# Two chained attention blocks on one core: the value product turned, the MLP computed by rows

## The reference, cut to what matters

```python
# block 0 (8 heads of 16, 64 sampled keys per image)
x_ln = layernorm(x);  q = x_ln @ wq + bq
# q -> depthwise conv 7x7 stride 2 -> gelu -> offsets -> bilinear sampling of x
k = v = interp @ wv + bv
attn = softmax(heads(q @ mq_w) . heads(k @ mk_w))          # 256 x 64 per head
att  = attn . heads(v @ mv_w)
z    = (att @ mo_w + mo_b) + x
x1   = gelu(layernorm(z) @ mlp_w + mlp_b) + z               # exact gelu
# block 1
xg = groupnorm(x1, 32 groups)                               # statistics over pixels and 4 channels
q, k, v = xg @ wq, xg @ wk, xg @ wv                         # + biases
out = softmax(q k^T / sqrt(128)) v @ wo + bo + x1
```

## Time and profile before

| | |
|---|---|
| median of 3 executions | 72.55 us (72.22 to 74.87) |
| the profiled execution's own time | 73.03 us |
| its span, first to last instruction | 71.2 us |
| granted TensorE clock | 1.00 |
| PE busy | 92% |
| PEld busy | 75% |
| DVE busy | 66% |
| ACT busy | 53% |
| POOL busy | 28% |
| HBM read, written | 2.42 MB, 0.52 MB |

### The profile page before, as it was taken

One profiled execution on the slowest core, in us unless ns is written; L12 is line 12 of the kernel. 1 busy time (PEld: TensorE's weight loads), 2 busy tenths in 40 slices (PEclk: granted clock), 3 DMA queues, 4 the chain that ended last, 5 costly groups with the idle time before them and its releaser, 6 DMA issues.

```text
span 71.2 us, 2063 instructions
## 1 busy us (share of the span) xinstructions
PE 65.6 (92%) x774; PEld 53.1 (75%) x774; DVE 47.0 (66%) x164; ACT 37.6 (53%) x94; POOL 19.9 (28%) x32
## 2 busy tenths in 40 slices
PE   4989789999999999999999999969999999999940
PEld 1316379987867758899889899738888889989730
DVE  0249873105523996679799998899499595375680
ACT  5210349544625686644441598973452949668400
POOL 6001999991000003960000931090300300000000
DMA  0778692000000000000000000000000000002213
GB/s 0 201 238 212 204 390 115 9 0 9 0 9 0 0 0 0 5 0 9 0 0 0 5 9 0 0 0 0 0 0 0 0 9 5 0 0 74 71 49 101
DMA packets 3051, 3.07 MB, mean 43 GB/s; under 512 B 225, under 2 KB 2657, under 8 KB 3042
## 3 DMA queue, kind: packets, MB, share of 16 engines
q1 hardware_dynamic: 3042, 2.95, 13.2%
HBM read 2.42 MB, written 0.52 MB: 41 GB/s over the span
## 4 chain that ended last, share of the span: by engine, by line
PE 83%; DVE 6%; DMA 4%; issue 2%; SPq 1%; DVEq 0%
PE bank L913 47%; PE score L913 22%; PE bank L1095 6%; DMA pack_early<-early 4%; PE score L1245 1%; PE bank L1113 1%; DVE y L779 1%; SPq L268 1%; DVE q_conv L579 1%; PE bank L1245 1%; DVE rec L777 1%; PE score L1164 1%; PE bank L1134 1%; DVE z L698 1%; PE score L1143 1%
## 5 line engine op out<-in xcount | busy, mean ns | idle before, releaser
L913 PEld LDWEIGHTS bank<-v_blk,p_t 128*128 128x128 f32 x64 | 7.8, 192 | 0.9 <-ACT p_t L446 0.7
L913 PE MATMUL bank<-v_blk,p_t 128*128 128x34 f32 x64 | 8.1, 272 | 0.0
L662 DVE TENSOR_REDUCE smax<-score 128x8 f32<-128x512 f32 x8 | 5.5, 686 | 1.6 <-PE score L913 1.6
L446 ACT ACTIVATE p_t<-bank 128x512 f32<-128x512 f32 x8 | 4.8, 599 | 2.7 <-PE bank L1095 2.7
L337 POOL TENSOR_TENSOR zrs<-zve,neg_half 128x2 f32<-128x2 f32 x4 | 2.8, 708 | 12.1 <-DVE zve L710 11.9
L913 PE MATMUL bank<-q_ph,wd 128*32 128x84 f32 (+5 forms) x256 | 6.0, 248 | 0.0
L913 PE MATMUL score<-warm 128*128 128x512 bf16 x12 | 5.0, 561 | 1.0 <-POOL warm L290 1.0
L913 PEld LDWEIGHTS bank<-q_ph,wd 128*32 128x32 f32 x256 | 5.3, 110 | 0.6 <-issue 0.3
L669 DVE TENSOR_TENSOR s_sub<-score,smax 128x512 f32<-128x512 f32 x8 | 5.5, 690 | 0.2
L324 POOL TENSOR_TENSOR x_res<-x_st,msa_bias 128x1024 f32<-128x1024 f32 x1 | 2.4, 2372 | 11.7 <-DVE bilin L642 11.7
L301 POOL TENSOR_TENSOR wd<-pack_early 128x512 f32<-128x512 f32 x4 | 4.1, 1047 | 5.2 <-DVE x_hat L602 5.2
(11 more groups left out here) (186 smaller groups left out, 162.6 us busy)
## 6 DMA issues: line engine op xcount, KB each, us to landing
x_st<-x SPq DMA_DIRECT2D x1, 512.0 KB, 7.3
pack_late<-late SPq DMA_DIRECT2D x1, 448.0 KB, 7.9
out<-y SPq DMA_DIRECT2D x3, 128.0 KB, 1.7
pack_fold<-fold SPq DMA_DIRECT2D x1, 320.0 KB, 4.5
pack_mid<-mid SPq DMA_DIRECT2D x1, 258.0 KB, 6.4
x_hw<-x SPq DMA_DIRECT2D x2, 128.0 KB, 2.6
x_hw<-x SPq DMA_DIRECT2D x1, 256.0 KB, 4.2
pack_early<-early SPq DMA_DIRECT2D x1, 184.0 KB, 2.9
```

Of the source, the lines that this page charges most:

```text
L446: act.activation(p_t[:, i % 2].rearrange("p j q -> p (j q)"), tile_bank(i)[:, :], ACT.Exp).then_inc(s["exp_ok"], 1)
L662: dve.tensor_reduce(smax[:, i % 2].rearrange("p (j e) -> p j e", e=2), scores, AX.X, ALU.max).then_inc(s["smax_ok"], 1)
L913: return pe.matmul(o, l, r_, start=start, stop=stop, **k)
```

## The change

1. **Value product turned.** The value blocks (32 columns) become the stationary operand and `p_t` (128 columns) the moving one; the four head pairs go to four quadrants of 32 partitions. Four more matmuls with a stationary mask of ones give the softmax sums, spread over the same layout. The result has channels on partitions, so `att_transpose` and its copy go. The reciprocal becomes `exp(-ln(sum))` on ACT, in a table set that holds both, loaded once by name where the Exp set was loaded.
2. **MLP by rows.** The weights are centred (`centre @ mlp_wg`), so z itself is multiplied: z is transposed, copied, and is the stationary operand, 128 columns of weights move. The row scale and the bias come after the product (`mlp_rows`, DVE), gelu follows on rows. `zhat_image`, `z_offset` and `zhat_transpose` go.
3. **Gelu transposed onto z.** z's transpose stays in PSUM as an open accumulation; `x1_add` transposes gelu onto it. `x1_image` and `x1_transpose` go; statistics and `norm_image` read PSUM.
4. **Residual rows on POOL** (`residual_rows`, `x1_rows`), in place of `x1_residual` on DVE.
5. **Bias rows** arrive by one broadcast transfer of 192 KB and are added by DVE; the two matmuls against a row of ones that added them go.
6. Group norm: one matmul where there were three ahead of the square; each image has its own bank for MLP, projections and x1; all engines' orders are rewritten.

The core of the diff (the order of each engine's steps is shown from the last tiles of the first attention on; ahead of that the new PE order is score 0, coord 1, query 1, score 1, transposes 0, residual bias, value 0, score 2, sample 1, transposes 1, key 1, score 3, values 1, value 1, transposes 2, score 4, out 0 and 1, value 2, transposes 3, score 5, `centre_weights`, value 3, `fold_second`, score 6, out 2, transposes 4, out 3, transposes 5, score 7):

```diff
             sp.dma_start(packs["mid"][:, :], mid).then_inc(s["mid_in"], 16)
+            sp.dma_start(biases[:, :, :].rearrange("p n c -> p (n c)"), bias_rows.partition_broadcast(P)).then_inc(s["biases_in"], 16)
             sp.dma_start(x_st[:, :, :], x_st_dram).then_inc(s["xst_in"], 16)
             sp.dma_start(packs["late"][:, :], late).then_inc(s["late_in"], 16)
 
+            def residual_rows(b):
+                pool.wait_ge(s["z_ok"], 2 * b + 2)
+                pool.wait_ge(s["outbias_ok"], 1)
+                pool.tensor_tensor(z_out[:, 2 * b:2 * b + 2], z[:, 2 * b:2 * b + 2], out_bias[:, :].unsqueeze(1).to_broadcast([P, S, C]),
+                                   ALU.add).then_inc(s["zout_ok"], 1)
+
+            def x1_rows(b):
+                pool.wait_ge(s["zout_ok"], b + 1)
+                pool.wait_ge(s["gel_ok"], b + 1)
+                pool.tensor_tensor(x1_res[:, 2 * b:2 * b + 2], z_out[:, 2 * b:2 * b + 2], gel[:, 2 * b:2 * b + 2], ALU.add).then_inc(s["x1res_ok"], 1)
...
             z_scale(2)
+            residual_rows(0)
+            residual_rows(1)
             z_scale(3)
             gn_pow(0)
+            x1_rows(0)
+            x1_rows(1)
+            residual_rows(2)
+            residual_rows(3)
             gn_pow(1)
+            x1_rows(2)
+            x1_rows(3)
...
+            def log_tile(i):
+                act.wait_ge(s["av_mm"], i + 1)
                 if i >= 2:
-                    act.wait_ge(s["msa_mm"], i - 1)
-                act.copy(att_t[:, i % 2], tile_bank(i)[:, ATT_T]).then_inc(s["attt_ok"], 1)
+                    act.wait_ge(s["inv_ok"], i - 1)
+                act.activation(log_sum[:, i % 2], tile_bank(i)[:, SUM], ACT.Ln).then_inc(s["log_ok"], 1)
+
+            def inverse_tile(i):
+                act.wait_ge(s["log_ok"], i + 1)
+                if i >= 2:
+
+                    act.wait_ge(s["att_ok"], i - 1)
+                act.activation(inv_sum[:, i % 2], log_sum[:, i % 2], ACT.Exp, scale=-1.0).then_inc(s["inv_ok"], 1)
...
+                act.activation(gel[:, 2 * b:2 * b + 2], mlp_in[:, 2 * b:2 * b + 2], ACT.Gelu).then_inc(s["gel_ok"], 1)
...
-            att_tile(4)
+            log_tile(4)
+            inverse_tile(4)
+            log_tile(5)
+            inverse_tile(5)
             exp_tile(6)
-            zhat_image(0)
             exp_tile(7)
-            zhat_image(1)
-            att_tile(5)
-            act.activation(scratch[:, 3:4], eps[:, :], ACT.Gelu)
             zt_image(0)
             zt_image(1)
+            log_tile(6)
+            log_tile(7)
+            inverse_tile(6)
+            inverse_tile(7)
+            act.activation(scratch[:, 3:4], eps[:, :], ACT.Gelu)
             gelu_image(0)
             gelu_image(1)
-            zhat_image(2)
-            out_bias_copy()
             zt_image(2)
             zt_image(3)
             gelu_image(2)
...
-            def recip_tile(i):
...
             def norm_tile(i):
-                dve.wait_ge(s["recip_ok"], i + 1)
+                dve.wait_ge(s["inv_ok"], i + 1)
...
+                dve.tensor_tensor(att_t[:, i % 2], tile_bank(i)[:, ATT], inv_sum[:, i % 2], ALU.mult).then_inc(s["att_ok"], 1)
...
+            def mlp_rows(i):
+                dve.wait_ge(s["mlp_mm"], i // S + 1)
+                dve.wait_ge(s["zrs_ok"], i // S + 1)
+                dve.wait_ge(s["mlpbias_ok"], 1)
+                dve.scalar_tensor_tensor(out=mlp_in[:, i], in0=image_bank(i // S)[:, i % S * C:(i % S + 1) * C], scalar=zrs[:, i:i + 1],
+                                         in1=mlp_bias[:, :], op0=ALU.mult, op1=ALU.add).then_inc(s["mlpin_ok"], 1)
...
+            def gn_mean(n):
+                i = slice(GN_SETS[n].start, GN_SETS[n].stop)
+                dve.wait_ge(s["dev_mm"], n + 1)
+                dve.tensor_tensor(gmean[:, i], gmv[:, i, 0], gn_bank(n)[:, DEV][:, i], ALU.subtract).then_inc(s["gmean_ok"], 1)
...
+            max_tile(7)
+            shift_tile(7)
+            z_aggr(1)
             z_stats(2)
-            z_tile(3)
             norm_tile(4)
-            max_tile(7)
+            norm_tile(5)
...
+            z_var(0)
             z_var(1)
+            z_tile(5)
...
+            mlp_rows(0)
             z_var(2)
+            norm_tile(6)
+            mlp_rows(1)
+            norm_tile(7)
+            mlp_rows(2)
+            mlp_rows(3)
             z_tile(6)
+            z_stats(6)
+            out_bias_out()
             z_tile(7)
-            z_stats(6)
-            z_stats(7)
-            z_aggr(6)
-            z_aggr(7)
-            z_offset(2)
-            z_var(3)
-            x1_image(0)
-            x1_image(1)
             gn_stats(0)
             gn_stats(1)
             gn_aggr(0)
             gn_aggr(1)
-            zhat_image(3)
+            z_aggr(6)
+            z_stats(7)
+            z_aggr(7)
+            z_var(3)
             gn_square(0)
+            gn_mean(0)
+            mlp_rows(4)
+            mlp_rows(5)
             gn_var(0)
+            mlp_rows(6)
+            mlp_rows(7)
             norm_image(0)
-            x1_residual(1)
             norm_image(1)
-            x1_image(2)
-            x1_image(3)
             gn_stats(2)
             gn_stats(3)
             gn_aggr(2)
             gn_aggr(3)
             query_out(0)
+            gn_mean(1)
+            gn_square(1)
             query_out(1)
-            gn_square(1)
-            x1_residual(2)
-            x1_residual(3)
             gn_var(1)
             norm_image(2)
+            max_image(0)
             norm_image(3)
-            max_image(0)
             max_image(1)
             query_out(2)
             query_out(3)
...
+                for at, stationary in ((ATT, v_blk[:, b]), (SUM, None)):
+                    for j in range(PAIRS):
+                        v = w("ones_mask") if stationary is None else stationary[:, j]
+                        m = mm(tile_bank(i)[j * VW:(j + 1) * VW, at], v, p_t[:, i % 2, j])
...
+                pe.wait_ge(s["ssub_ok"], T)
                 for t in range(S):
-                    m = pe.transpose(zt_bank(b)[:, HW + t * P:HW + (t + 1) * P], z[:, 2 * b + t], w("ident"))
+                    m = mm(x1_cols(b)[:, t * P:(t + 1) * P], z[:, 2 * b + t], w("ident"), start=(t == 0), stop=False, is_transpose=True, skip_group_check=True)
                 m.then_inc(s["zr_mm"], 1)
...
+                pe.wait_ge(s["mlpwc_ok"], 1)
+                for t in range(S):
+                    m = mm(image_bank(b)[:, t * C:(t + 1) * C], z_t[:, 2 * b + t, :], mlp_wc[:, :], start=False, skip_group_check=True)
+                m.then_inc(s["mlp_mm"], 1)
...
+            def x1_add(b):
+
+                pe.wait_ge(s["gel_ok"], b + 1)
                 for t in range(S):
-                    m = pe.transpose(bank[3 + b][:, HW + t * P:HW + (t + 1) * P], x1_t[:, b, t * P:(t + 1) * P], w("ident"))
-                m.then_inc(s["x1rows_mm"], 1)
+                    m = mm(x1_cols(b)[:, t * P:(t + 1) * P], gel[:, 2 * b + t], w("ident"), start=False, is_transpose=True, skip_group_check=True)
+                m.then_inc(s["x1_mm"], 1)
+
+            def gn_apart(n):
                 i = slice(GN_SETS[n].start, GN_SETS[n].stop)
                 pe.wait_ge(s["gmv_ok"], i.stop)
                 if n == 0:
...
+                mm(gn_bank(n)[:, DEV][:, i], w("group_rest"), gmv[:, i, 0]).then_inc(s["dev_mm"], 1)
...
+            score_tile(7)
             value_tile(4)
+            value_tile(5)
             transpose_scores(6)
-            att_transpose(4)
-            value_tile(5)
+            z_transpose(0)
+            transpose_scores(7)
             out_project(4)
-            transpose_scores(7)
+            z_transpose(1)
+            out_project(5)
             value_tile(6)
-            att_transpose(5)
+            mlp_image(0)
+            mlp_image(1)
+            z_transpose(2)
             out_project(6)
             out_project(7)
             output_bias()
-            gn_mean(0)
+            x1_add(0)
+            x1_add(1)
+            z_transpose(3)
+            mlp_image(2)
+            gn_apart(0)
+            mlp_image(3)
             gn_spread(0)
+            x1_add(2)
+            x1_add(3)
             project_k(0)
             project_q(0)
+            project_k(1)
+            gn_apart(1)
             project_q(1)
-            x1_transpose(2)
-            x1_transpose(3)
-            project_k(1)
-            gn_mean(1)
             project_v(0)
             gn_spread(1)
             score_image(0)
             score_image(1)
+            project_v(1)
             project_q(2)
```

More of the change, by code:

```diff
@@ L23 @@
 PIX = OH * OW
-VW = 2 * HD + 2
+VW = 2 * HD
 LN_EPS, GN_EPS = 1e-5, 1e-6
@@ L66, with build @@
 PLACE = {pack: columns(parts) for pack, parts in PACKS.items()}
-def build(nc, x, early, fold, mid, late, rows, ln_rows, out):
+def build(nc, x, early, fold, mid, late, rows, ln_rows, bias_rows, out):
     ctx = ExitStack()
@@ L187, in build @@
```

(41 more changed lines are left out.)

392 lines of the change are left out of this document (164 added, 228 removed).

## The result

| | before | after |
|---|---|---|
| median of 4 executions each | 72.64 us (72.22 to 74.87) | 75.17 us (75.09 to 76.48) |
| ratio, 95% interval | | 1.033 [1.028, 1.038] |
| span of the profiled execution | 71.2 us | 73.0 us |
| its own time | 73.03 us | 75.16 us |
| granted TensorE clock | 1.00 | 0.95 |

The forecast was 69.8 us within 67.6 to 72.4. Of most kernels here single executions are some per cent slower than the rest, mostly at a lower clock; ratios leave them out, medians don't, and where a kernel has no ratio its lowest time is given.

The account below looks back on a forecast made before the run. It saw a loop set by a single score buffer, then serial chains, then dense PE work, rather than PE alone. Stage gains took 2.7 us off the 71.2 us span; from the 72.55 median this gave 69.8 us, range 67.6 to 72.4.

Parts of the forecast that it names:

- the one on POOL: Residual rows on POOL: eight operations of 256 columns at 0.61, 4.9 us, hidden if the powers behind them are not late.
- the term for tile 2: First attention: value product 0, the bilinear step and the bias sums hold DVE until 27.9 instead of 28.2.
- The slower rival (ACT's order): First attention: logs ahead of later exps delay each exp and stall the loop, 6.4 us over 6 tiles; 74.7 us, 7%.
- Packed value product: First attention on PE: turned product of 16 instructions takes 0.55 us per tile instead of 0.82, saving 3.4 us with att's transpose.
- the second rival: Score loop on PE: changeovers of packing, 0.11 us paid twice per tile, add 1.8 us; 71.6 us, 20%.
- Work of the engines: Whole kernel: PE loses 5.6 us of work, DVE ends about 3 us lighter, POOL gains 4.9 us.
- ACT's chain: After the first attention: exp, copies, log, inverse and an exposed 1.28 us table load lead to gelu at 45.3; gain 1.5.
- The power of the second half: Second group norm on POOL: `gn_pow(1)` stands behind four residual operations until 52.3, in time by 1.2 us.
- Loop: First attention's score rounds, set by a single score buffer: 2.21 us each, last subtraction ending at 40.3 instead of 41.5.
- The same work in another order: Stretch up to the first scores: only reordered, so they come at 22.4 instead of 22.45.
- Outside the span: Time of the profiled execution beyond its span: 1.8 us, kept unchanged.

Follow-up runs that it names:

- e1: The changed kernel with POOL's wait for the second bilinear step put back ahead of `x_res`; 71.67 us, ratio 0.986 to the kernel before.
- e3: The kernel before with only POOL's wait for the second bilinear step ahead of `x_res` taken out; 76.42 us, ratio 1.035.
- e11: The changed kernel, no wait put back, with `x_res` made in four operations of 256 columns instead of one of 1024; 72.58 us, ratio 0.991.

## Why the prediction was wrong

**The step that failed** is the one on POOL. The prediction costed POOL's eight new operations (4.9 us, hidden) and nothing else of that engine's list. That `x_res` no longer waited for the bilinear product was not in it, as a gain or as a risk, nor which DVE operation would run beside it. In the sum this is the term for tile 2: there the bilinear step and the bias sums were to hold DVE until 27.9, and they held it until 30.2, because the bilinear step took 2.56 us and not the 0.42 that it had before (29.94 + 0.28; 28.20 in e1). And no term allowed for a slower clock. That is 2.1 us of stall and 2.1 us of clock, 4.1 of the 4.5 us between the forecast span of 68.5 and the measured 73.0. The slower rival (ACT's order) gave 74.7, near the time that came, but only by chance; it is not what happened: only the two rounds in the hole and the slow clock are above 2.4 us (27.22 to 32.59 to 36.02), and behind them the rounds are 2.25, 2.21 and 2.38, in e1, with ACT's order the same, 2.32, 2.21 and 2.38. The Trainium skill states the rule in SBUF — State Buffer (Who interferes with whom): a DVE instruction with two SBUF inputs contends with a GpSimd one that reads SBUF. It calls this an exclusive lock, and says of DVE's two-port modes that the other engine blocks for the whole instruction; the traces show that for this pair too, 0.28 or 0.29 us between the two ends in four traces.

**The rest of the path came within 0.5 us of the forecast,** read in e1, where the collision is absent; times are of the profiled executions:

| stage | before | forecast | e1 | after |
|---|---|---|---|---|
| first scores | 22.45 | 22.4 | 22.78 | 22.66 |
| last subtraction ends | 41.52 | 40.3 | 40.81 | 44.89 |
| gelu of image 0 | 46.76 | 45.3 | 45.64 | 49.73 |
| first normalized image | 51.49 | 50.0 | 50.20 | 54.27 |
| image 2 normalized | 56.96 | 54.5 | 54.70 | 58.77 |
| scores of images 0 and 1 done | 57.64 | 54.9 | 55.29 | 59.36 |
| span | 71.2 | 68.5 | 68.9 | 73.0 |

The lines of the changed kernel behind the last column, DVE, ACT and PE, which answer to the earlier trace rows:

```profile
44.20 0.69 DVE L704 TENSOR_TENSOR s_sub<-score,smax 128x512 f32<-128x512 f32 x1
...
54.27 0.99 DVE L783 TENSOR_SCALAR x_gn<-score,gmean,grs 128x256 f32<-128x256 f32 x2 [0.32 <-POOL grs L351]
...
58.77 0.55 DVE L783 TENSOR_SCALAR x_gn<-score,gmean,grs 128x256 f32<-128x256 f32 x1 [0.89 <-POOL grs L351]
```
```profile
47.80 0.50 ACT L489 ACTIVATE inv_sum<-log_sum 128x128 f32<-128x128 f32 x2
48.32 1.28 ACT L576 ACT_TABLE_LOAD   x1
...
49.73 0.71 ACT L497 ACTIVATE gel<-mlp_in 128x256 f32<-128x256 f32 x2
```
```profile
57.55 1.97 PE L930 MATMUL bank<-k,q 128*128 128x256 f32 x8
59.36 0.61 PE L930 MATMUL bank<-w_vog,x_gn 128*128 128x128 f32 x4
```

Point by point:

- *Packed value product, 0.55 forecast, bounds 0.45 and 1.81.* It is 0.46, next to the lower bound. PE, products of tiles 4 and 5 in the changed kernel:

```profile
43.29 0.42 PE L930 MATMUL bank<-p_t,v_blk 128*32 128x128 f32 x8
43.53 0.40 PE L930 MATMUL bank<-p_t,pack_mid 128*32 128x128 f32 x8
43.75 0.40 PE L930 MATMUL bank<-p_t,v_blk 128*32 128x128 f32 x8
43.97 0.40 PE L930 MATMUL bank<-p_t,pack_mid 128*32 128x128 f32 x8
44.30 0.66 PE L1116 MATMUL bank<-pack_early,s_sub 128*128 128x128 f32 x4
```

  From start to start 0.24, 0.22, 0.22, 0.33: a product alone 0.46, and 0.11 more where full transposes follow, as much as the second rival priced a changeover. Whether it is one was not tested; with it the product costs 0.57 at most, the forecast's 0.55, and the rival's extra 1.8 us is not there: the loop of e1 is 0.1 us longer than forecast, see below.
- *Work of the engines.* e1's page, against the earlier trace rows:

```profile
PE 61.6 (89%) x820; PEld 47.3 (69%) x820; DVE 45.0 (65%) x152; ACT 36.7 (53%) x95; POOL 25.3 (37%) x39
```

  PE has 4.0 us less where 5.6 were counted, DVE 2.0 less where 3 were, POOL 5.4 more where 4.9 were. The missing 1.6 of PE are not traced to single products, and as busy times of pipelined matmuls they are rough.
- *ACT.* Log 0.28 as assumed, inverse 0.31. One table load ahead of the first exp (24.37) and the one ahead of gelu, in the open with ACT's chain intact (47.80, 48.32, 49.73), as forecast; logs and exps alternate with no load between. The chain came 0.3 late.
- *POOL.* A residual operation of 256 columns takes 0.70 to 0.73, not 0.61. The power of the second half still comes in time.
- *DVE.* Normalizing from PSUM takes 0.54 where it took 0.41 from SBUF; not in the sum, 0.1 on the path.
- *Loop.* Of the 0.5 us by which the last subtraction ends late in e1, 0.4 are there at the first scores already (22.78 against 22.4); the loop itself takes 18.03 against 17.9. "The same work in another order" was not free: from `move_half(1)` to the first scores it takes 8.65 us in e1 (22.78 − 14.13) and 7.65 before (22.45 − 14.80), of which the gap behind 109 tap products is 0.67. That the first scores are late by only 0.4 is luck: what lies ahead of `move_half(1)` was 0.67 shorter in that execution.
- *Outside the span* 1.8 was kept. e1's profiled execution took 71.40 us where 70.3 was forecast: 0.4 of it in the span, 0.7 outside.

So with its one wait the change does to the span most of what was forecast, 2.3 us of 2.7, and its time falls by 1.4%, not 4%.

## What to carry to other kernels

Read the removed waits of a diff like removed instructions: for each, write down which operation can now start earlier, and what on the neighbouring engine will run beside it. Look above all for a long GpSimd operation with SBUF inputs that can slide beside a short VectorE operation with two SBUF inputs on the critical path: here one wait, another order or smaller pieces cured it. A stall of TensorE is priced with the slower clock that may follow; here that doubled it, in the profiled execution of e3 it did not come.

## What the runs showed of the hardware

- DVE's `scalar_tensor_tensor` with two SBUF inputs, 0.42 us alone, took 2.56, 2.57, 2.13 and 0.95 beside POOL's `tensor_tensor` on SBUF, ending 0.28 or 0.29 us behind that instruction (in the last case behind the first of four) each time. POOL's long one was not slower (2.34 against 2.37).
- PE idled for 2.34 us in dense work. The granted clock fell to 0.5 (1.2 GHz, from 2.4) 1.5 us into it, at about 29.3 us, and was full again at about 36.1, at a cost of 2.1 us. After 0.73 us of idling in e11, and after 1.65 in the profiled execution of e3, it stayed full there, so the length of the idle time alone does not decide it.
- Behind 109 packed tap products without a pause PE stands idle for "issue": 0.40 us in the changed kernel, 0.67 in e1, nothing where 88 are followed by others. Length alone is not the cause: image 0's 128 tap products (11.79 to 14.51 in the changed kernel) run through without such a stop. The cause was not tested further.
